# Expert products of 512 columns issued as two halves of 256, in a four-block attention and expert kernel

## What is computed

```python
x = x + _L0_xattn_ref(_layernorm(x), ctx, ctx, mask, ...)
x = x + _L0_ffn_ref(_layernorm(x), ...)
x = x + _L1_xattn_ref(_layernorm(x), ctx, bias, ...)
x = x + _L1_ffn_ref(_layernorm(x), ...)

# _L1_ffn_ref(x): H = 8 heads, E = 8 experts, P = D = 128
xv  = einsum('bsd,hedp->bshep', x, v_w)         # every token through all 64 value experts
v   = einsum('bshep,bshe->bhsp', xv, gate_v)    # gated sum, 2 of 8 per head
att = softmax(einsum('bhqp,bhkp->bhqk', q, k) * SCALE)
ctx = einsum('bhqk,bhkp->bqhp', att, v)
out = einsum('bshep,hepd->bsd', ctx[:, :, :, None, :] * gate_o[..., None], o_w)
```

## Time and profile before

| | |
|---|---|
| median of 3 runs | 1483.1 us (1482.65 to 1484.07) |
| span of the profiled execution | 1482.2 us |
| PE busy | 1419.3 us, 96% of the span, 9905 matmuls |
| PE weight loads | 961.5 us, 65% |
| DVE busy | 1323.1 us, 89% |
| ACT busy | 1276.0 us, 86% |
| POOL busy | 858.9 us, 58% |
| granted clock of PE | 0.978 on average |

### The profile page before, as it was taken

How to read it: one execution, slowest core, us unless ns; L and a number is a source line. 1 busy time by engine, 2 the same in 40 slices (tenths; PEclk the granted TensorE clock), 3 DMA queues, 4 the chain that set the end, 5 groups by cost and what they waited for, 6 DMA issues and landing times.

```text
span 1482.2 us, 34265 instructions
## 1 busy us (share of the span) xinstructions
PE 1419.3 (96%) x9905; PEld 961.5 (65%) x9905; DVE 1323.1 (89%) x4498; ACT 1276.0 (86%) x4428; POOL 858.9 (58%) x1345
## 2 busy tenths in 40 slices
PE   4678999999999999999999999999999999999998
PEld 2355666666666666666666666666666666666654
DVE  3677999999999999999999999999999999999986
ACT  3657888999988899998889999888899988889886
POOL 3112656566565666656566666656556565655667
PEclk8589999999999999999999999999999999999999
DMA  5420000000000000000000000000000000000000
GB/s 135 138 56 16 8 16 16 14 15 12 16 8 16 16 14 15 13 16 9 16 16 15 15 13 16 9 16 16 15 14 13 15 9 16 14 15 7 8 3 4
DMA packets 68954, 30.13 MB, mean 20 GB/s; under 512 B 19168, under 2 KB 68768, under 8 KB 68768
## 3 DMA queue, kind: packets, MB, share of 16 engines
q1 hardware_dynamic: 51552, 19.31, 4.9%
q10 hardware_dynamic: 17216, 8.65, 2.1%
HBM read 17.31 MB, written 2.10 MB: 13 GB/s over the span
## 4 chain that ended last, share of the span: by engine, by line
PE 89%; DVE 3%; POOL 2%; ACT 2%; issue 2%; DMA 1%; SPq 1%; POOLq 0%; DVEq 0%
PE psC L308 58%; PE psA L308 13%; PE psB L308 7%; PE psB L532 4%; PE psC L628 2%; PE psA L420 1%; PE psB L552 1%; PE psA L465 1%; POOL TE L3428 1%; POOL accO L3440 1%; ACT PTB L1343 1%; DVE TE L2500 1%; POOL v_sb L3433 0%; SPq L3811 0%; DVE nmA L2239 0%
## 5 line engine op out<-in xcount | busy, mean ns | idle before, releaser
L3440 POOL TENSOR_TENSOR accO<-accO,TE 128x512 f32<-128x512 f32 x192 | 246.4, 1283 | 147.1 <-DVE TE L2500 140.9
L1343 ACT ACTIVATE TE<-psC,gateO 128x128 f32<-128x128 f32 x1024 | 292.6, 375 | 24.6 <-PE psC L308 16.4
L1343 ACT ACTIVATE TE<-psC,gate 128x128 f32<-128x128 f32 x1024 | 297.0, 394 | 17.7 <-PE psC L308 10.4
L2500 DVE SCALAR_TENSOR_TENSOR TE<-psC,gate,TE 128x128 f32<-128x128 f32 x1024 | 284.7, 340 | 29.1 <-PE psC L308 19.4
L2500 DVE SCALAR_TENSOR_TENSOR TE<-psC,gateO,TE 128x128 f32<-128x128 f32 x1024 | 287.2, 342 | 12.5 <-PE psC L308 8.0
L3428 POOL TENSOR_TENSOR TE<-TE 128x256 f32<-128x256 f32 x256 | 192.1, 751 | 164.2 <-DVE TE L2500 159.4
L308 PE MATMUL psC<-Vh,xTh 128*128 128x512 f32 x512 | 264.6, 517 | 2.2 <-ACT PS L1343 1.2
L308 PE MATMUL psC<-Oh,ch 128*128 128x512 f32 x512 | 262.4, 513 | 0.7 <-DVE TE L2500 0.6
L308 PE MATMUL psC<-Oh,cl 128*128 128x512 f32 x512 | 203.1, 397 | 0.0
L308 PE MATMUL psC<-Vh,xTl 128*128 128x512 f32 x512 | 202.7, 396 | 0.0
L308 PE MATMUL psC<-Vl,xTb 128*128 128x512 bf16 x512 | 199.9, 390 | 0.0
(11 more groups left out here) (228 smaller groups left out, 3449.4 us busy)
## 6 DMA issues: line engine op xcount, KB each, us to landing
bdB<-Kc SPq DMA_DIRECT2D x384, 16.0 KB
raw<-in_L_ffn_v_w ACTq DMA_DIRECT2D x8, 512.0 KB, 4.4
raw<-in_L_ffn_o_w ACTq DMA_DIRECT2D x8, 512.0 KB, 4.0
x_sb<-in_x SPq DMA_DIRECT2D x32, 64.0 KB, 2.1
ctx_sb<-in_ctx SPq DMA_DIRECT2D x32, 64.0 KB, 2.0
bdA<-Kc SPq DMA_DIRECT2D x128, 8.0 KB
Qb<-Qc SPq DMA_DIRECT2D x128, 8.0 KB
bias_sb<-in_mask_Bx1xSxS_ff SPq DMA_DIRECT2D x32, 64.0 KB, 2.0
```

The lines of the kernel that those rows point to most:

```text
L1343: return A.activation(o, i, func, **kw)
L2500: m = V.scalar_tensor_tensor(TE[:, i, e], psC[:, p, e * P:(e + 1) * P], gates[:, e:e + 1], TE[:, i, e], ALU.mult, ALU.add)
L3440: G.tensor_tensor(accO[:], TE[:, slot(b, H1)] if h == 1 else accO[:], TE[:, slot(b, H1 + h)], ALU.add).then_inc(o_fe, 1)
```

## The change

In `experts` the three passes are made over columns 0 to 255 of the half bank, and then over columns 256 to 511. Each pass has its own weight load, as before, so that each of the three stationary operands is loaded twice per product. The wait in front of the first pass and the signal on the last one stay. The readers of the bank are unchanged.

```diff
                 e0 = h * NE + half * HALF
                 wh, wl = flat(w_hi[:, e0:e0 + HALF]), flat(w_lo[:, e0:e0 + HALF])
                 pe.wait_ge(*free[half])
-                mm(o, hi, wh, True, False)
-                mm(o, lo, wh, False, False)
-                mm(o, low, wl, False, True).then_inc(done, 1)
+                for c in (0, 256):
+                    part = slice(c, c + 256)
+                    mm(o[:, part], hi, wh[:, part], True, False)
+                    mm(o[:, part], lo, wh[:, part], False, False)
+                    m = mm(o[:, part], low, wl[:, part], False, True)
+                m.then_inc(done, 1)
```

## The result

| | before | after |
|---|---|---|
| median | 1483.6 us (1482.65 to 1484.81) | 1506.3 us (1505.61 to 1507.07) |
| ratio | | 1.015, 95% interval 1.0138 to 1.0162 |
| span of the profiled execution | 1482.2 us | 1505.3 us |
| PE busy / weight loads busy | 1419.3 / 961.5 us | 1439.3 / 1227.9 us |
| DVE / ACT busy | 1323.1 / 1276.0 us | 1327.0 / 1282.0 us |

Both were measured side by side, so the kernel before stands at 1483.6 here. The change costs 22.7 us. I had forecast 48.4: the sign and the range (1495 to 1546) held, the size did not. The first rival, by the column, had said 1500.

The account below looks back on a forecast made before the run. PE's own stream was taken to bound the kernel: 17.4 us for the bf16 passes plus 41.0 for the float32r passes minus 10 regained from waits gave +48.4, so 1531.5 us, range 1495 to 1546.

Parts of the forecast that it names:

- The first rival, by the column: Float32r passes: excess goes with columns, instructions add only 5.5 us; +17 us in all, 1500 us (1495 to 1507); chance 25%.
- The bound: Steady middle: PE is busy 39.98 to 39.99 of 40 us, so whatever is added to its stream is added to the time.
- The bf16 pass: Low pass behind float32r: its load starts only with its own matmul; 0.017 x 1024 = 17.4 us, bounds 10 to 20.
- by the instruction: Float32r passes hi and lo: each added matmul costs the whole 0.020 us excess, 2048 x 0.020 = 41.0 us.
- My own sign of being wrong: The forecast is wrong if the distance of float32r ends is halved, or PE shows new gaps behind DVE or ACT.
- both arguments: Float32r excess: nearly low's size, suggesting a cost per instruction; exact at half clock, 0.42 per 512 columns, suggesting limited supply.
- No rate per column other than one or two clocks is seen: Float32r passes: reason given for charging 0.020 us to each instruction, 41.0 us, instead of to the columns.
- What hides the new loads: Weight loads under 256-column streams: 0.107 plus the excess just covers a load of 0.11; costed at nothing.
- What comes back: PE's waits for ACT in the middle shrink as PE comes later: 10 us back of 58, or 6 of 23.
- Only an instruction step: All passes: low's load is hidden too, and 3072 x 0.0027 = 8.3 us is all; 1491 us; chance 3%.
- Faster: Float32r passes of 256 columns take 0.110 each, faster below 0.1125; -10 us, 1473 us; chance 7%.
- the first two cases: Float32r excess charged per instruction, about 1520 to 1545 us, 58%; or per column, 1495 to 1507 us, 25%.

Follow-up runs that it names:

- the unsplit bf16 kernel: Kernel before with hi and lo using low's bf16 operands, so all three passes are bf16 at 512 columns: 1442.0 us, ratio 0.9713.
- the bf16 kernel: Changed kernel (256-column halves) with hi and lo using low's bf16 operands, so all three passes are bf16: 1447.1 us, ratio 0.975.
- the two kernels that take transitions out: Changed kernel with low first over the right 256 columns, 1493.9 us; kernel before with low first in the left half's product, 1476.2 us.

## Why the prediction was right or wrong

**The bound: right.** PE's stream is the time. The chain's dense pieces changed by 0.027 per product, a batch by 0.72, and 32 batches by the 23 us measured. In the windows of the middle (640 to 720 us) PE is busy for 39.92 of 40 us.

**The bf16 pass: right in kind, a little low.** I had 17.4 us for 1024 more low passes behind float32r, and 20 as the upper bound; by pairs the low pass of a product went from 231 to 2 x 126 ns, 21 us. Moving half of the low passes away gave 12.4 us back in the split kernel and 8.0 for 512 of them in the unsplit one, 0.012 and 0.016 a time, and the halves behind one another cost 3.3 us in all. The load that isn't issued ahead and the price came together in every timeline; no run has the one without the other, so that the load is the cause is my reading.

**The float32r passes: the step that failed.** It is the term "by the instruction: 0.020 each, 41.0 us". Split alone they cost 2.2 us, and in the change 3 to 6 (what is left of 24 to 27 beside low's 21), so the excess of 0.020 goes with the columns, as the four sizes show. My own sign of being wrong came: the distance of float32r ends was halved, from 235 to 117 ns. I had both arguments on the page and chose by the weaker: the excess of float32r and that of low were nearly equal in size (0.020 and 0.018), and I took this for a common cause. It was chance. A row that leaned the other way was there: at the lower clock two float32r passes end 0.42 apart, their columns at 1.2 GHz and nothing on top. A limit per column gives that. It does not decide, though, for a price per instruction can vanish at the lower clock as well, and the trace of the kernel before shows one that does. Here are its bf16 passes of 128 columns at a granted clock of 0.50 (a window, five passes, and the last one of them alone):

```profile
26.60:27.50 0.90, 0.82 (x8) 0.55 (x6) 0.90 (x2) 0.53 (x2) 0.00 (x0) 0.50 0.07 19
26.68 0.74 PE L308 MATMUL psA<-Q,bdA 128*128 128x128 bf16 x5
27.10 0.31 PE L308 MATMUL psA<-Q,bdA 128*128 128x128 bf16 x1
```

(0.74 - 0.31)/4 is 0.107 each, in the trace 106 to 107 ns, where 128/1.2 is 106.7. At 1.00 the same passes are 56 ns apart for 53.3 of columns, and these 0.003 belong to the instruction, as 109 ns for 256 and 216 for 512 show. Only float32r at another size could settle it, and the kernel before has none. "No rate per column other than one or two clocks is seen" was no argument either, as float32r was seen at one size only.

**What hides the new loads: right, and close to its edge.** At 256 columns float32r passes end 0.12 apart with a load of 0.11 under each; behind a low pass of 256, which streams for 0.109, hi takes 119 ns for 116 to 117 elsewhere. At 128 the load shows, +0.05 a time.

**What comes back: about right in kind.** I had 10 of 58 us; it was 1 to 4 of 24 to 27. That the waits absorb a part is shown by the unsplit bf16 kernel, where 0.05 x 1024 = 51 us less work on PE gave 42.5 us, and new idle time behind ACT stands in the waits.

**The sum with what was measured by parts:** 2.2 (float32r), 3.3 (the low pass being two) and 12.4 to 16 for 1024 low passes placed behind float32r, where the run gives 12.4 and the price of 0.0156 gives 16. That is 18 to 21.5 of the 22.7. The intervals of the comparisons, each 1.3 to 2 us to either side, could hide the rest, but the pairs assign most of it: hi behind a low pass of 256 stands once in every product of the change, and twice where a product follows a product. It never stands in the kernel with only the float32r passes split, and costs some 0.003 a time, 4 us in all as an estimate.

**The rivals.** The first (by the column: 17 us, 1500) was the right mechanism, 6 us too low: its low pass was 17.4 where 21 was paid, and it took back 6 where 1 to 4 came back. "Only an instruction step" is refuted with float32r and is about what the bf16 kernel does (5.1 us for 3072 instructions). "Faster" is refuted: 0.117 to 0.119 is above its turning point of 0.1125. My weights of 58 to 25% between the first two cases were too far apart for what the rows could tell.

## What to carry to other kernels

When an excess is to be put down to the instruction or to the column, look for it at another size before choosing; another clock is weaker evidence, since a small price per instruction can vanish there too. If no row has another size, leave both readings near even chances. On PE count transitions between operand types as well as instructions: put the bf16 passes of neighbouring float32r products side by side, and let a product behind a short step begin with the pass whose weights load quickest. Splitting a float32r stream was nearly free at 256 columns, where a stream still covers the next weight load (2.2 us for 2048 passes), and dear at 128.

## What the runs showed of the hardware

- Float32r streams at some 0.46 ns per column at a granted clock of 1.00 for 128, 256, 384 and 512 columns (59, 117, 176 and 235 ns), where bf16 takes 0.42 (1.89 for eight passes of 512); at 0.50 it takes 0.42 us for 512, with nothing on top. That a supply of four bytes per column is what limits it is my reading; no run shows it.
- The weight load of a bf16 pass is issued ahead behind a bf16 pass and not behind a float32r one; the transition costs 0.016 us by pairs, at 256 columns (126 for 109 ns) and at 512 (231 for 216), and 0.012 to 0.016 by the times of the two kernels that take transitions out.
- A float32r weight load takes 0.11 us before its matmul can stream (lo ends 111 ns behind a hi of 128 columns). A stream of 256 columns covers it but for some 0.003, one of 128 leaves 0.05 to be seen. The Trainium skill ("TensorE: Matmul & The Clock Gate", "The mechanism") says that a load overlaps a matmul in flight only when its row group differs. By that sentence no load of all 128 rows would overlap; the traces disagree, as float32r loads of 0.11 stay hidden under streams of 256 columns that end 0.117 apart.
